# Down products that add to y in PSUM, with y put there by ScalarE or by TensorE, in place of sums on GpSimd

## The chip, the cores and the metric

The kernel runs on one core of one Trainium2 chip. The metric is the device time of one execution in microseconds (us), the median of several runs.

## What is computed

A graph network (two relational convolutions over 625 nodes of 768 features) is followed by a block with 16 experts and one shared network. Only the second part is touched by the change. Cut to what matters:

```python
y = silu(h @ sg_w) * (h @ su_w) @ sd_w            # shared network, 1536 wide
for i in range(16):
    gate_feature = h * pe[i] @ gate_w + gate_b    # 625 x 768
    gate_weight, gate_idx = top_k(gate_feature, 384)
    gate_weight = softmax(gate_weight)
    gathered = take_along_axis(h, gate_idx)
    y = y + (silu((gathered * gate_weight) @ eg_w[i]) * (... @ eu_w[i])) @ ed_w[i]
out = silu(layernorm(y) @ m1_w + m1_b) @ m2_w + m2_b
```

All of it is in float32. The 625 tokens lie as 5 tiles of 125 rows, so y is a tile `y_tok` of 125 x 5 x 768.

## The kernel before

**The sort sets the order.** The top 384 of 768 with what goes with them (the payload: the values of h at those places) come out of a sorting network. The function `experts` runs an OPENING, then 15 REGULAR turns (turn 1 apart, turns 2 to 14 as a hardware loop, turn 15 apart), then a CLOSING. A REGULAR turn has 93 units. In the first 38 or so, units of the new expert's sort of halves alternate with units of the previous expert's merge of the top. In turn 7, the turn that is read most below, unit 0 begins at 3479.6 us. A unit compares two sides of up to 960 columns:

- ScalarE copies the first side into a PSUM bank (`seed`, L1507).
- VectorE takes the larger keys (L1616) and the smaller ones (L1626).
- TensorE subtracts the larger keys from that bank (L1218), so the bank becomes a mask.
- VectorE moves the first payload under the mask (L1649) and the second (L1666). The second one is shared. VectorE moves its part from a saved copy (`pay_side`, made by ScalarE at L1520). For the other part GpSimd adds both sides beforehand (`add_pays`, L1319) and subtracts the new first side afterwards (`take_pays`, L1327).

**How much GpSimd takes** is the function `shares`: half of the payload in a woven unit, 6 of 8 parts where the unit is in `REGULAR.free`, and 3 of 8 in the last units. `REGULAR.free` holds the units beside which GpSimd has nothing else to do, by the list `asked_early` and `asked_late`. The cut goes along the first dimension longer than 1, so where that dimension is 2 the share stays a half whatever is asked.

**Products beside the sort.** While a turn sorts, TensorE also makes 125 x 384 or 128 x 313 products in two PSUM slots (`slots`), spread over the units by their column counts: after the mask of a unit it makes the product parts placed there. The work on a product's result follows one unit later on ScalarE and two later on GpSimd. Engines take their instructions in order, so a long product part delays the next unit's mask. In a loop turn the first half of the units has the 10 down products of the expert before last (`expert_out`: 6 matmuls each, in two parts) and gate products, and the second half the hidden products of the last expert. The shared network is cut in 4 pieces (`piece`): piece 0 in the OPENING, 1 in turn 1, 2 in turn 15, and 3 in the CLOSING and after it. A piece's down products have 3 matmuls each. Turn 15 also holds the down products of experts 13 and 14; those of expert 15 come at the very end.

**y before.** A down product starts at zero. ScalarE copies it out to `y_part`, which lies in `u_feat` (`summed`, L1446), and GpSimd adds that to `y_tok` (`add_to_y`, L1287). There are 10 per expert and 10 per piece, 200 in all. `y_tok` starts from a memset.

Of the kernel before, what the change touches and what calls it, by code (L numbers as in the profile page):

```python
# [819 lines left out]
def experts(nc, ffn, chunks, ident, neg_ident, ones, pe_t, h_tok, h_feat, y_tok, gate_w, gate_b, gate_loaded,  # L820
            m1_loaded):
    with ExitStack() as ctx:
# [3 lines left out]
        def sem(name):  # L826
            return ctx.enter_context(nc.semaphore(name))
# [33 lines left out]

        def is_set(e, t):

            return t < AHEAD and not (isinstance(e, int) and e == 0)
# [30 lines left out]
        y_part = u_feat[:, :, :].rearrange("p k c -> p (k c)")[0:TP, 0:D].rearrange("p (h x) -> p h x", h=2)  # L895
# [14 lines left out]
        hid_ready, y_added = sem("hid_ready"), sem("y_added")  # L910
# [152 lines left out]
        asked_early = [asked(True, parts) for parts in down_parts(KD)]  # L1063
# [52 lines left out]
        def _(pe):  # L1116
# [41 lines left out]
            def down(n, bank, t, half, nf, down_w, loads, hids, part):  # L1158
                if part == 0:
                    if hids is not None:  # L1160
                        pe.wait_ge(hid_ready, hids + 1)
                        pe.wait_ge(down_loaded, loads * 16)
                    room(n)
                for f in range(part * KK, part * KK + KK):
                    last = pe.matmul(slots[bank][0:TP, 0:HALF], hid[:, f, t * TP:(t + 1) * TP],  # L1165
                                     down_w[:, f, half * HALF:(half + 1) * HALF], start=(f == 0), stop=(f == nf - 1))
                if part == nf // KK - 1:
                    last.then_inc(filled, 1)
# [11 lines left out]
            def downs(base, nf, down_w, loads, hids):  # L1180
                return [(down, (base + n, n % 2, t, half, nf, down_w, loads, hids if n == 0 else None), parts)
                        for n, (t, half, parts) in enumerate(halves_of(down_parts(nf)))]
# [8 lines left out]
            def expert_out(e, base):  # L1191
                return downs(base, KD, w_exp, before(e, 1, 1) + 1, before(e, NGU, SGU) + NGU)
# [6 lines left out]
            def piece_out(q, base):  # L1199
                return downs(base + 2 * SGU, KK, w_piece_down, before_piece(q, 1, 1) + 1,  # L1200
                             before_piece(q, NGU, SGU) + SGU)
# [63 lines left out]
        def _(pool):  # L1265
# [32 lines left out]
            def downs(base, nf):  # L1298
                return [(add_to_y, (base + n, t, half), parts) for n, (t, half, parts) in enumerate(halves_of(down_parts(nf)))]
# [4 lines left out]
            def expert_out(base):  # L1304
                return downs(base, KD)

            def piece(base):
                return hiddens(base, KD, KK) + [PAUSE] + downs(base + 2 * SGU, KK)
# [54 lines left out]
            pool.memset(y_tok[:, :, :], 0.0).then_inc(y_added, 1)  # L1363
            pool.wait_ge(y_added, 1)
# [10 lines left out]
            with pool.Fori(2, NEXP - 1) as i:  # L1375
                base = LOOP_BASE + (i - 2) * PER_TURN
                begin_gate(i + 1)
                sort(REGULAR, i, beside_all(
                    REGULAR, expert_out(base) + gate_products(i + 1, range(AHEAD)),
                    expert_in(base + (NHALF + NEARLY)) + gate_products(i + 1, range(AHEAD, NT)), 2))  # L1380
            sort(REGULAR, NEXP - 1, beside_all(REGULAR, expert_out(LAST_BASE) + piece(LAST_BASE + NHALF),
                                               expert_in(LAST_IN) + [PAUSE] + expert_out(LAST_IN + NIN), 2))
# [4 lines left out]
            now(downs(CLOSE_BASE + 2 * SGU, KK))  # L1387
            now(expert_in(END_BASE))
            now(expert_out(END_BASE + NIN))

        @block.scalar
        def _(act):
            def turned(n, bank, ys, t, first, last):
                if t == 0:
                    act.wait_ge(y_added, ys + 1)
# [17 lines left out]
            def with_biases(products):  # L1413


                if products[0][0] is take_feat:
                    for n, bank, _, _, half in [args for _, args, _ in products[0:2]]:
                        set_bias(n, bank, half)
                todo = []
                for n, (work, args, parts) in enumerate(products):  # L1420
                    later = products[n + 2] if n + 2 < len(products) else None
                    if later is not None and later[0] is take_feat and is_set(*later[1][2:4]):
                        todo.append((both, ((work, args), (set_bias, (later[1][0], later[1][1], later[1][4]))), parts))
                    else:
                        todo.append((work, args, parts))
                return todo
# [30 lines left out]
            def downs(base, nf, ys):  # L1457
                return [(summed, (base + n, n % 2, ys, t, half), parts)
                        for n, (t, half, parts) in enumerate(halves_of(down_parts(nf)))]

            def expert_in(e, base):
                turns = [(turned, (base + n, n % 2, before(e, NHALF, NHALF), *place), parts)
# [3 lines left out]
            def expert_out(e, base):  # L1466
                return downs(base, KD, before(e, NHALF, NHALF))
# [4 lines left out]
            def piece_out(q, base):  # L1472
                return downs(base + 2 * SGU, KK, before_piece(q, NHALF, NHALF))
# [101 lines left out]
            for work, args, _ in gate_products(0, NHALF):  # L1575
# [3 lines left out]
            sort(OPENING, 0, beside(OPENING, with_biases(gate_products(1, PIECES) + piece(0, OPEN_BASE)), 1, 1,  # L1579
                                    OPENING.n - 6), REGULAR)  # L1580
            sort(REGULAR, 1, beside_all(
                REGULAR, with_biases(gate_products(2, SECOND_BASE, range(AHEAD)) + piece(1, SECOND_BASE + NEARLY)),
                with_biases(expert_in(0, SECOND_IN) + gate_products(2, SECOND_IN + NIN, range(AHEAD, NT))), 1), REGULAR)
            with act.Fori(2, NEXP - 1) as i:
                base = LOOP_BASE + (i - 2) * PER_TURN
                sort(REGULAR, i, beside_all(
                    REGULAR, with_biases(expert_out(i - 2, base) + gate_products(i + 1, base + NHALF, range(AHEAD))),
                    with_biases(expert_in(i - 1, base + (NHALF + NEARLY))
                                + gate_products(i + 1, base + (NHALF + NEARLY + NIN), range(AHEAD, NT))), 1), REGULAR)
            sort(REGULAR, NEXP - 1, beside_all(  # L1590
                REGULAR, expert_out(NEXP - 3, LAST_BASE) + piece(2, LAST_BASE + NHALF),
# [239 lines left out]
```

## Time and profile before

| what | value |
| --- | --- |
| median of 3 runs | 6728.27 us (6721.94 to 6728.85) |
| span of the profiled execution | 6726.6 us |
| TensorE busy | 5752.0 us, 86% |
| VectorE busy | 5167.5 us, 77% |
| GpSimd busy | 4158.4 us, 62% |
| ScalarE busy | 2659.1 us, 40% |
| first REGULAR turn begins | 1552.4 us |
| last REGULAR turn ends | 6396.5 us |

The profiled execution has no time of its own beside its span, which lies 1.7 us under the median. TensorE's float32 matmuls appear as two records each, so a product of 6 matmuls reads as x12. Matmul ends are modelled, and busy time over the whole span mixes stages with different limits.

### The profile page before, as it was taken

The page shows a single profiled execution, that of the slowest core. Times are in us where ns is not written, and L with a number is a line of the kernel's source. Part 1 is how long each engine was busy: PE and PEld are TensorE (multiplying, and loading weights), DVE is VectorE, ACT ScalarE, POOL GpSimd, SP SyncE. Part 2 cuts the span into 40 slices and gives each one's busy share as a digit, 9 for nine tenths or more (in the row PEclk, how much of TensorE's full clock was granted, in tenths as well). Part 3 has the DMA queues.
Part 4 walks back from the last instruction along what each step waited for, and adds up shares of the span by engine and source line. Part 5 has one row for each costly group of instructions (what it writes and reads, how often), then busy time and mean ns, then how long its engine had stood idle before and what let it go on. Part 6 is the DMA issues. An engine that isn't in the chain of part 4 may idle for free. (4 is left out here: it accounts for less than half of the span.)

```text
span 6726.6 us, 73995 instructions
## 1 busy us (share of the span) xinstructions
PE 5752.0 (86%) x16753; PEld 3063.2 (46%) x16753; DVE 5167.5 (77%) x6633; ACT 2659.1 (40%) x4419; POOL 4158.4 (62%) x3692
## 2 busy tenths in 40 slices
PE   7979989788888888888888888888888888889988
PEld 5545545344444444444444444444444444445554
DVE  3012002399999999999999999999999999998840
ACT  0000000244545554454545454545454545554431
POOL 2325005266877777676777777777777777777740
PEclk9989999899999999999999999999999999999989
DMA  3357238100000000000000000000000000001001
GB/s 90 107 132 188 101 99 196 56 15 8 20 23 15 15 15 15 15 15 15 15 15 14 15 14 15 15 19 10 29 0 29 14 15 15 15 29 36 18 32 51
DMA packets 118084, 261.01 MB, mean 39 GB/s; under 512 B 39164, under 2 KB 49922, under 8 KB 117682
## 3 DMA queue, kind: packets, MB, share of 16 engines
q1 hardware_dynamic: 70322, 180.18, 7.6%
q0 software_dynamic: 47360, 77.17, 5.2%
q14 instruction: 357, 2.92, 0.1%
q8 instruction: 45, 0.74, 0.0%
HBM read 222.43 MB, written 34.58 MB: 38 GB/s over the span
## 5 line engine op out<-in xcount | busy, mean ns | idle before, releaser
L1218 PE MATMUL mask_ps<-key,neg_ident 125*125 125x480 f32 (+7 forms) x4128 | 1886.1, 575 | 567.4 <-DVE key L1626 561.2
L1327 POOL TENSOR_TENSOR pay<-pay_side,pay 125x480 int32<-125x480 int32 (+9 forms) x1120 | 1306.1, 1166 | 648.1 <-DVE pay L1649 641.0
L1507 ACT COPY mask_ps<-key 125x960 f32<-125x960 f32 (+7 forms) x1152 | 954.7, 829 | 1698.7 <-DVE pay L1666 1029.3
L1319 POOL TENSOR_TENSOR pay_side<-pay 125x480 int32<-125x480 int32 (+9 forms) x1120 | 1301.1, 1162 | 340.6 <-DVE pay L1666 160.9
L1218 PEld LDWEIGHTS mask_ps<-key,neg_ident 125*125 125x125 f32 x4128 | 732.8, 192 | 1459.8 <-DVE key L1626 994.5
L1649 DVE COPY_PREDICATED pay<-mask_ps,pay 125x960 f32<-125x960 int32 (+6 forms) x1120 | 1240.7, 1108 | 69.0 <-PE mask_ps L1218 35.5
L1616 DVE TENSOR_TENSOR key<-mask_ps,key 125x960 f32<-125x960 f32 (+6 forms) x1120 | 1092.4, 975 | 57.5 <-PE mask_ps L1218 36.2
L1626 DVE TENSOR_TENSOR key<-mask_ps,key 125x960 f32<-125x960 f32 (+6 forms) x1120 | 1092.8, 976 | 0.0
L1218 PE MATMUL mask_ps<-key_top,neg_ident 125*125 125x480 f32 (+3 forms) x1472 | 604.1, 539 | 178.2 <-DVE key_top L1626 168.0
L1165 PE MATMUL slot_ps<-w_exp,hid 128*125 128x384 f32 x1920 | 680.4, 493 | 8.7 <-issue 8.7
L1153 PE MATMUL slot_ps<-gate_w,xs 128*125 128x384 f32 x1920 | 678.8, 490 | 0.0
L1137 PE MATMUL slot_ps<-u_feat,w_exp 128*128 128x312 f32 (+1 forms) x2304 | 668.2, 427 | 0.4 <-ACT u_feat L1397 0.4
L758 POOL DMA_INDIRECT rows_a<-messages_dram,idx_now_a x200 | 242.3, 1212 | 660.6 <-DVE idx_now_a L795 612.7
L657 PE MATMUL ps_msg<-w_rel,h_feat 128*125 128x384 f32 x1920 | 619.7, 486 | 2.4 <-ACT h_feat L589 2.4
L1666 DVE COPY_PREDICATED pay<-mask_ps,pay_side 125x480 f32<-125x480 int32 (+8 forms) x1120 | 592.1, 529 | 4.8 <-DVE pay L1649 2.9
L1520 ACT COPY pay_side<-pay 125x480 f32<-125x480 f32 (+8 forms) x1120 | 508.6, 454 | 147.0 <-POOL pay L1327 97.6
L1137 PEld LDWEIGHTS slot_ps<-u_feat,w_exp 128*128 128x128 f32 x2304 | 439.7, 191 | 245.0 <-issue 119.0
L668 DVE COPY y_out<-ps_msg 125x768 f32<-125x768 f32 x40 | 38.3, 958 | 612.2 <-PE ps_msg L657 612.2
L1165 PEld LDWEIGHTS slot_ps<-w_exp,hid 128*125 128x125 f32 x1920 | 366.4, 191 | 306.9 <-issue 114.7
L1327 POOL TENSOR_TENSOR pay_top<-pay_side,pay_top 125x480 int32<-125x480 int32 (+3 forms) x272 | 327.5, 1204 | 281.1 <-DVE pay_top L1649 276.8
L1153 PEld LDWEIGHTS slot_ps<-gate_w,xs 128*125 128x125 f32 x1920 | 359.1, 189 | 306.1 <-issue 120.8
L1218 PEld LDWEIGHTS mask_ps<-key_top,neg_ident 125*125 125x125 f32 x1472 | 270.8, 199 | 489.1 <-DVE key_top L1626 289.7
(190 smaller groups left out, 5876.3 us busy)
## 6 DMA issues: line engine op xcount, KB each, us to landing
w_rel<-L_gnn_W SPq DMA_DIRECT2D x16, 2304.0 KB, 23.2
w_exp<-L_ffn_ed_w SPq DMA_DIRECT2D x16, 2304.0 KB, 8.4
messages_dram<-y_out SPq DMA_DIRECT2D x16, 1875.0 KB
w_exp<-L_ffn_eg_w SPq DMA_DIRECT2D x16, 1152.0 KB, 5.4
w_exp<-L_ffn_eu_w SPq DMA_DIRECT2D x16, 1152.0 KB, 7.8
root_w<-L_gnn_root SPq DMA_DIRECT2D x2, 2304.0 KB
w_exp<-L_ffn_sg_w SPq DMA_DIRECT2D x4, 1152.0 KB, 6.0
w_exp<-L_ffn_su_w SPq DMA_DIRECT2D x4, 1152.0 KB, 8.8
```

The source lines that it names most:

```text
L657: last = pe.matmul(slots[n % 2][0:TP, half, 0:HALF], h_feat[:, k, t * TP:(t + 1) * TP], w_rel[j][:, k, cols], start=(k == 0), stop=(k == K ...
L1137: last = pe.matmul(slots[bank][:, 0:count], weight(bank, k), ins[:, k, first:first + count], start=(k == 0), stop=(k == nk - 1))
L1153: last = pe.matmul(slot, xs[:, t % 2, k, :], gate_w[:, k, cols], start=False, stop=(k == KD - 1), skip_group_check=is_set(e, t))
L1165: last = pe.matmul(slots[bank][0:TP, 0:HALF], hid[:, f, t * TP:(t + 1) * TP], down_w[:, f, half * HALF:(half + 1) * HALF], start=(f == 0), ...
L1218: last = pe.matmul(mask, neg_ident[0:TP, 0:TP], operand, start=False, stop=True, skip_group_check=True)
L1319: pool.tensor_tensor(shares(pay_was(turn, u), turn, u)[1].bitcast(I32), first, second, ALU.add).then_inc(pays_added, 1)
L1327: pool.tensor_tensor(second, shares(pay_was(turn, u), turn, u)[1].bitcast(I32), first, ALU.subtract).then_inc(pays_taken, 1)
L1507: act.copy(seed_of(turn, u), compared(turn, u)[0]).then_inc(seeded, 1)
L1616: dve.tensor_tensor(results(turn, u)[0], seed_of(turn, u), compared(turn, u)[1], ALU.max).then_inc(maxed, 1)
L1626: dve.tensor_tensor(smaller, seed, second, ALU.min).then_inc(minned, 1)
L1649: dve.copy_predicated(larger, mask_of(turn, u), second).then_inc(moved, 1)
L1666: dve.copy_predicated(smaller, mask, was).then_inc(pays_done, 1)
```

## The change

A down product now adds onto y in its PSUM slot and ScalarE copies the sum back to `y_tok` (`summed`). How y gets into the slot depends on the product:

- For experts 0 to 13 (`y_is_set`), ScalarE copies y into the slot (`set_y`, L1418 of the changed kernel) right after it has emptied the slot two products earlier. The first two copies of a turn stand ahead of the turn's first unit.
- For pieces 1 to 3 and experts 14 and 15 (`ADDED`), TensorE puts it there by one more matmul at the head of each product: an identity times `y_tok` (L1172).
- Piece 0 (`FIRST`) starts y, so the memset goes.

GpSimd's `add_to_y` is removed, and its entries in `asked_early` no longer keep a unit out of `REGULAR.free`.

```diff
-        y_part = u_feat[:, :, :].rearrange("p k c -> p (k c)")[0:TP, 0:D].rearrange("p (h x) -> p h x", h=2)
...
-        asked_early = [asked(True, parts) for parts in down_parts(KD)]
+        asked_early = [asked(False, parts) for parts in down_parts(KD)]
...
+        def y_is_set(e):
+            return not (isinstance(e, int) and e >= NEXP - 2)
...
                     room(n)
+                    if y is ADDED:
+                        pe.matmul(slot, ident[0:TP, 0:TP], y_tok[:, t, cols], start=True, stop=False)
+                    elif y is not FIRST:
+                        pe.wait_ge(y_set, y + (2 * t + half + 1))
                 for f in range(part * KK, part * KK + KK):
...
+                                     start=(f == 0 and y is FIRST), stop=(f == nf - 1),
...
-            def add_to_y(n, t, half):
-                cols = slice(half * HALF, (half + 1) * HALF)
-                pool.wait_ge(emptied, n + 1)
-                pool.tensor_tensor(y_tok[:, t, cols], y_tok[:, t, cols], y_part[:, half, :], ALU.add).then_inc(y_added, 1)
...
-            pool.memset(y_tok[:, :, :], 0.0).then_inc(y_added, 1)
...
+            def set_y(n, bank, t, half):
+                act.wait_ge(emptied, n - 1)
+                act.copy(slots[bank][0:TP, 0:HALF], y_tok[:, t, half * HALF:(half + 1) * HALF]).then_inc(y_set, 1)
...
-            def summed(n, bank, ys, t, half):
+            def summed(n, bank, t, half, is_y_set):
                 act.wait_ge(filled, n + 1)
-                act.wait_ge(y_added, ys + max(2 * t + half, 1))
-                act.copy(y_part[:, half, :], slots[bank][0:TP, 0:HALF]).then_inc(emptied, 1)
+                act.copy(y_tok[:, t, half * HALF:(half + 1) * HALF], slots[bank][0:TP, 0:HALF]).then_inc(emptied, 1)
```

Ten units of a REGULAR turn enter `REGULAR.free`: 5, 7, 10, 12, 15, 17, 21, 24, 26 and 28. Four of them keep their shapes (5, 7 and 15 are cut along a dimension of 2, and 17 has no second payload). The other six change. VectorE's queue in the loop, at the second payloads of units 24 and 26, stands so before:

```order
L1616 TENSOR_TENSOR key_top<-mask_ps,key_top 125x6x160 [waits mask_made,seeded]
L1666 COPY_PREDICATED pay_top<-mask_ps,pay_side 125x320 [waits moved]
L1626 TENSOR_TENSOR key_top<-mask_ps,key_top 125x6x160 [waits maxed]
L1645 REGISTER_ALU [waits mask_made]
L1647 REGISTER_ALU [waits pay_copied]
L1649 COPY_PREDICATED pay<-mask_ps,pay 125x8x120 [waits pays_added]
L1608 REGISTER_ALU
L1616 TENSOR_TENSOR key<-mask_ps,key 125x8x60 [waits mask_made,seeded]
L1666 COPY_PREDICATED pay<-mask_ps,pay_side 125x4x120 [waits moved]
```

The same piece of VectorE's queue in the changed kernel:

```order
L1626 TENSOR_TENSOR key_top<-mask_ps,key_top 125x6x160 [waits mask_made,seeded]
L1676 COPY_PREDICATED pay_top<-mask_ps,pay_side 125x320 [waits moved]
L1636 TENSOR_TENSOR key_top<-mask_ps,key_top 125x6x160 [waits maxed]
L1655 REGISTER_ALU [waits mask_made]
L1657 REGISTER_ALU [waits pay_copied]
L1659 COPY_PREDICATED pay<-mask_ps,pay 125x8x120 [waits pays_added]
L1618 REGISTER_ALU
L1626 TENSOR_TENSOR key<-mask_ps,key 125x8x60 [waits mask_made,seeded]
L1676 COPY_PREDICATED pay<-mask_ps,pay_side 125x2x120 [waits moved]
```

Nothing has moved. VectorE's second copy of unit 26 goes from 480 to 240 columns, and nothing else in its queue changes but that kind of copy: unit 10 and unit 28 from 240 to 120, units 12, 24 and 26 from 480 to 240, and unit 21 from 320 to 160.

TensorE's queue in turn 15, at down products of expert 14 (`slot_ps<-w_exp,hid`) between masks, before:

```order
L1165 MATMUL slot_ps<-w_exp,hid 125x384 [waits emptied]
L1165 MATMUL slot_ps<-w_exp,hid 125x384 x5
L1218 MATMUL mask_ps<-key,neg_ident 125x4x120 [waits minned]
L1218 MATMUL mask_ps<-key,neg_ident 125x3x120
L1165 MATMUL slot_ps<-w_exp,hid 125x384 [waits emptied]
L1165 MATMUL slot_ps<-w_exp,hid 125x384 x2
```

The same place in the changed kernel:

```order
L1172 MATMUL slot_ps<-y_tok,ident 125x384 [waits emptied]
L1176 MATMUL slot_ps<-w_exp,hid 125x384 x6
L1231 MATMUL mask_ps<-key,neg_ident 125x4x120 [waits minned]
L1231 MATMUL mask_ps<-key,neg_ident 125x3x120
L1172 MATMUL slot_ps<-y_tok,ident 125x384 [waits emptied]
L1176 MATMUL slot_ps<-w_exp,hid 125x384 x3
```

Each product has become one matmul longer, and the mask behind it stands behind that matmul too.

ScalarE's queue at the start of a loop turn, before:

```order
L1507 COPY mask_ps<-key_top 125x640 [waits pays_done]
L1544 REGISTER_ALU
L1496 COPY pay<-h_tok 125x256x5 [waits kept]
L1496 COPY pay<-h_tok 125x128x10 [waits pays_done]
L1496 COPY pay<-h_tok 125x128x10
```

The same place in the changed kernel:

```order
L1418 COPY slot_ps<-y_tok 125x384 [waits emptied]
L1417 REGISTER_ALU
L1418 COPY slot_ps<-y_tok 125x384 [waits emptied]
L1513 ISA
L1514 ISA [waits maxed]
L1516 REGISTER_ALU [waits minned]
L1517 COPY mask_ps<-key_top 125x640 [waits pays_done]
L1554 REGISTER_ALU
L1506 COPY pay<-h_tok 125x256x5 [waits kept]
L1506 COPY pay<-h_tok 125x128x10 [waits pays_done]
L1506 COPY pay<-h_tok 125x128x10
```

Two copies of y now stand ahead of the seed of unit 1 and the three copies that lay out the new payload.

## Rows read from the trace of the kernel before

**Rows 1.** The page, busy tenths of each engine in 40 equal slices.

```profile
DVE  3012002399999999999999999999999999998840
```

**Rows 2.** Turns 2, 7, 15, rest: length, PE PEld DVE ACT POOL busy, clock, DMA.

```profile
1877.80:2195.70 317.90, 268.21 (x753) 136.60 (x753) 307.24 (x372) 159.15 (x267) 235.53 (x207) 0.97 0.04 16
3479.60:3799.50 319.90, 268.45 (x753) 136.55 (x753) 307.15 (x371) 159.02 (x267) 236.53 (x208) 0.96 0.04 15
6045.70:6396.50 350.80, 318.41 (x953) 179.10 (x953) 308.91 (x372) 162.64 (x281) 252.82 (x227) 0.96 0.09 33
6396.50:6726.60 330.10, 275.62 (x881) 168.73 (x881) 91.55 (x110) 76.14 (x136) 75.77 (x77) 0.90 0.10 35
```

**Rows 3.** Waits of VectorE in turn 7, the longest in total: us, times, longest.

```profile
DVE key_top L1616 <- PE mask_ps L1218: 3.6, 2, 2.7
```

**Rows 4.** VectorE's second payload copies in turn 7, by shape.

```profile
L1666 DVE COPY_PREDICATED pay<-mask_ps,pay_side 125x480 f32<-125x480 int32 x17 | 12.0, 704 | 0.0
...
L1666 DVE COPY_PREDICATED pay<-mask_ps,pay_side 125x240 f32<-125x240 int32 x26 | 11.5, 441 | 0.3 <-DVE pay L1649 0.2
...
L1666 DVE COPY_PREDICATED pay<-mask_ps,pay_side 125x120 f32<-125x120 int32 x7 | 2.1, 295 | 0.0
...
L1666 DVE COPY_PREDICATED pay_top<-mask_ps,pay_side 125x320 f32<-125x320 int32 x3 | 1.6, 521 | 0.0
...
L1666 DVE COPY_PREDICATED pay_top<-mask_ps,pay_side 125x160 f32<-125x160 int32 x2 | 0.7, 334 | 0.0
```

**Rows 5.** Timeline of turn 7: TensorE, then VectorE, near units 27 to 29.

```profile
3574.43 1.77 PE L1218 MATMUL mask_ps<-key_top,neg_ident 125*125 125x480 f32 x4
...
3577.05 1.07 PE L1218 MATMUL mask_ps<-key,neg_ident 125*125 125x480 f32 x2 [0.85 <-DVE key L1626]
...
3576.90 1.26 DVE L1649 COPY_PREDICATED pay_top<-mask_ps,pay_top 125x960 f32<-125x960 int32 x1
...
3583.10 1.24 DVE L1649 COPY_PREDICATED pay_top<-mask_ps,pay_top 125x960 f32<-125x960 int32 x1 [0.24 <-issue]
```

**Rows 6.** GpSimd in turn 7, by shape.

```profile
L1327 POOL TENSOR_TENSOR pay<-pay_side,pay 125x480 int32<-125x480 int32 x15 | 18.1, 1204 | 9.1 <-DVE pay L1649 9.1
...
L1327 POOL TENSOR_TENSOR pay<-pay_side,pay 125x720 int32<-125x720 int32 x7 | 11.5, 1649 | 1.5 <-DVE pay L1649 1.5
...
L1287 POOL TENSOR_TENSOR y_tok<-y_tok,u_feat 125x384 f32<-125x384 f32 x10 | 10.0, 1002 | 0.0
```

**Rows 7.** ScalarE's copies out of and into a product slot, turn 7.

```profile
L1446 ACT COPY u_feat<-slot_ps 125x384 f32<-125x384 f32 x10 | 4.8, 478 | 3.7 <-PE slot_ps L1165 3.7
...
L1411 ACT COPY slot_ps<-bias_rows 125x384 f32<-125x384 f32 x8 | 3.9, 483 | 0.7
```

**Rows 8.** Busy time in stretches with down products, columns as in group 2.

```profile
1703.40:1737.90 34.50, 33.71 (x100) 18.50 (x98) 32.74 (x42) 20.11 (x40) 33.07 (x33) 0.98 0.00 1
...
6208.10:6244.30 36.20, 36.13 (x102) 19.93 (x102) 32.52 (x43) 20.93 (x39) 34.30 (x35) 0.92 0.00 1
...
6319.70:6357.60 37.90, 34.17 (x95) 17.02 (x94) 31.09 (x39) 14.12 (x25) 25.08 (x24) 1.00 0.00 1
...
6357.60:6388.10 30.50, 30.50 (x89) 16.27 (x87) 25.11 (x29) 12.22 (x21) 26.20 (x20) 1.00 0.01 2
```

**Rows 9.** Timeline after the last sort: TensorE, then the last two products.

```profile
6494.08 17.25 PE L1165 MATMUL slot_ps<-w_piece_down,hid 128*125 128x384 f32 x48 [6.58 <-ACT u_feat L1446]
...
6604.33 0.48 ACT L1446 COPY u_feat<-slot_ps 125x384 f32<-125x384 f32 x1 [3.39 <-PE slot_ps L1165]
...
6608.20 0.48 ACT L1446 COPY u_feat<-slot_ps 125x384 f32<-125x384 f32 x1 [3.39 <-PE slot_ps L1165]
...
6608.76 0.99 POOL L1287 TENSOR_TENSOR y_tok<-y_tok,u_feat 125x384 f32<-125x384 f32 x1 [2.88 <-ACT u_feat L1446]
```

**Rows 10.** Clock where turns 2 and 7 begin, columns as in group 2.

```profile
1872.00:1892.50 20.50, 12.82 (x20) 5.35 (x19) 17.04 (x21) 12.90 (x16) 8.33 (x7) 0.59 0.00 0
...
3476.30:3496.80 20.50, 12.76 (x18) 5.49 (x19) 15.19 (x17) 12.75 (x16) 6.99 (x6) 0.50 0.01 2
```

More of the change, by code:

```diff
@@ L860, in experts @@
         BEGIN = SCALE + NT
+        FIRST, ADDED = "first", "added"
+        def y_is_set(e):
+            return not (isinstance(e, int) and e >= NEXP - 2)
         def is_set(e, t):
@@ L1156, in gate, with down @@
                     last.then_inc(filled, 1)
-            def down(n, bank, t, half, nf, down_w, loads, hids, part):
+            def down(n, bank, t, half, nf, down_w, loads, hids, y, part):
+                cols = slice(half * HALF, (half + 1) * HALF)
+                slot = slots[bank][0:TP, 0:HALF]
                 if part == 0:
@@ L1163, in down @@
                     room(n)
+                    if y is ADDED:
+                        pe.matmul(slot, ident[0:TP, 0:TP], y_tok[:, t, cols], start=True, stop=False)
+                    elif y is not FIRST:
+                        pe.wait_ge(y_set, y + (2 * t + half + 1))
                 for f in range(part * KK, part * KK + KK):
-                    last = pe.matmul(slots[bank][0:TP, 0:HALF], hid[:, f, t * TP:(t + 1) * TP],
-                                     down_w[:, f, half * HALF:(half + 1) * HALF], start=(f == 0), stop=(f == nf - 1))
+                    last = pe.matmul(slot, hid[:, f, t * TP:(t + 1) * TP], down_w[:, f, cols],
+                                     start=(f == 0 and y is FIRST), stop=(f == nf - 1),
+                                     skip_group_check=y is not ADDED and y is not FIRST)
                 if part == nf // KK - 1:
@@ L1386, in _, with turned @@
                 weigh(NEXP - 1, t)
-            now(downs(CLOSE_BASE + 2 * SGU, KK))
             now(expert_in(END_BASE))
-            now(expert_out(END_BASE + NIN))
         @block.scalar
         def _(act):
-            def turned(n, bank, ys, t, first, last):
-                if t == 0:
-                    act.wait_ge(y_added, ys + 1)
+            def turned(n, bank, t, first, last):
                 act.wait_ge(filled, n + 1)
@@ L1411, in set_bias, with setting, with_settings @@
                 act.copy(slots[bank][0:TP, 0:HALF], bias_rows[:, half * HALF:(half + 1) * HALF]).then_inc(bias_set, 1)
[L1413 to L1418, printed above, removed]
+            def set_y(n, bank, t, half):
+                act.wait_ge(emptied, n - 1)
+                act.copy(slots[bank][0:TP, 0:HALF], y_tok[:, t, half * HALF:(half + 1) * HALF]).then_inc(y_set, 1)
+            def setting(work, args):
+                if work is take_feat and is_set(*args[2:4]):
+                    return [(set_bias, (args[0], args[1], args[4]))]
+                if work is summed and args[4]:
+                    return [(set_y, args[0:4])]
+                return []
+            def with_settings(products):
+                for work, args, _ in products[0:2]:
+                    do(setting(work, args))
                 todo = []
                 for n, (work, args, parts) in enumerate(products):
[L1421 to L1425, printed above, removed]
+                    sets = setting(*products[n + 2][0:2]) if n + 2 < len(products) else []
+                    todo.append((both, ((work, args), *sets), parts) if sets else (work, args, parts))
                 return todo
@@ L1455, in hiddens, with downs @@
                         for n, (place, parts) in enumerate(zip(places, mixed_parts(nk, nf)))]
-            def downs(base, nf, ys):
-                return [(summed, (base + n, n % 2, ys, t, half), parts)
+            def downs(base, nf, is_y_set):
+                return [(summed, (base + n, n % 2, t, half, is_y_set), parts)
                         for n, (t, half, parts) in enumerate(halves_of(down_parts(nf)))]
             def expert_in(e, base):
-                turns = [(turned, (base + n, n % 2, before(e, NHALF, NHALF), *place), parts)
+                turns = [(turned, (base + n, n % 2, *place), parts)
                          for n, (place, parts) in enumerate(zip(TURNS, turn_parts))]
```

44 lines of the change are left out of this document (22 added, 22 removed).

## The prediction, made before the changed kernel ran

> **What bounds the kernel now.** I read the page first. VectorE is busy nine tenths or more in nearly every slice from about 1500 us on [rows 1], and those slices are the 15 REGULAR turns. So I asked for busy time by turn. Turn 7 lasts 319.90 us, of which VectorE is busy 307.15 and TensorE 268.45; turn 15 lasts 350.80 with nearly the same VectorE time, 308.91, but TensorE 318.41; and in the 330.10 us after the last turn VectorE has only 91.55, TensorE 275.62 [rows 2]. The reader should see three regimes. A loop turn goes by VectorE. Turn 15 goes in part by TensorE, and so does the tail. In a loop turn the rest of VectorE's time, 12.75 us, is spent in a few waits; the largest is 3.6 us for masks at two places [rows 3], none of them on GpSimd's sums into y.
>
> **What the change saves on VectorE.** Six second payload copies per turn get shorter. By shape, 480 columns take 704 ns, 240 take 441, 120 take 295, and for the top 320 take 521 and 160 take 334 [rows 4]. Three units save 0.263 us each, two 0.146, one 0.187: 1.27 us per turn. Is all of it gained? Not quite, since TensorE is close behind. In turn 7 it works without a pause from unit 22 until the mask of unit 27, which ends at 3576.20 (3574.43 + 1.77); VectorE uses that mask at 3576.90, 0.70 us later [rows 5]. The savings of units 21, 24 and 26 lie ahead of that instruction and sum to 0.71. I take about 0.2 us as lost there, because a mask's end and its use never lie closer than some 0.2 us in the stretches where VectorE waits. The mask of unit 28 begins 0.85 us after TensorE fell idle, so the pause can take the shift [rows 5]. Unit 28's own 0.146 lies just ahead of an instruction that already waits 0.24 us, at 3583.10 [rows 5], and is lost. That leaves 0.92 us per turn, bounds 0.4 (nothing from units 21 to 28) and 1.27. Thirteen loop turns give 12.0 us, turns 1 and 15, where TensorE paces units 20 to 30, half of that each: **12.9 us gained**, bounds 5.2 and 19.
>
> **What it costs GpSimd and ScalarE.** A GpSimd sum goes from 1204 ns at 480 columns to 1649 at 720 [rows 6], twice per unit. I scale this by columns: the three large units cost 0.9 each, the others about 0.6 each, near 4.5 us per turn. Against that go ten sums into y of 1002 ns, 10.0 us [rows 6]. GpSimd ends 5 us lighter in a turn where it has 83 us of pause [rows 2], so I take nothing. What it costs if the cover fails is a rival below. ScalarE gets ten copies of y into a slot. The nearest row is the bias copied into the same slots, 483 ns; the copy out of it costs 478 and stays [rows 7]. That is 4.8 us per turn on an engine that is busy half of it. A copy of y stands right behind a copy out and ahead of the next seed, which itself waits for VectorE. At a turn's start two copies, 0.97 us, stand ahead of the seed of unit 1 and the three payload copies. VectorE waits there for masks anyway [rows 3]. I take nothing; the lower bound is also nothing, the upper bound 1 us per turn.
>
> **What it costs TensorE.** A down product of expert 15 is paced by TensorE: 6604.33 to 6608.20, 3.87 us for 6 matmuls of 384 columns, 0.645 us each [rows 9]. The added identity matmul has 384 columns too, so 0.645 us. There are 50, in five places:
>
> - Turn 1, piece 1, ten products: TensorE is busy 33.71 of 34.50 us [rows 8]. Ten cost 6.45. The pause of 0.8 and about 1.3 just behind it take some: **4.3** (2.5 to 6.45).
> - Turn 15, piece 2, ten products: 36.13 busy of 36.20 [rows 8], and then hidden products that also fill TensorE. **5.5** (4 to 6.45).
> - Turn 15, expert 14. Its first five products lie in 37.90 us with 34.17 busy, so 3.2 us find 3.73 of pause: nothing. The last five lie in 30.50 us with 30.50 busy [rows 8]: **3.2** (3.2 to 6.45).
> - Piece 3, after the sort: TensorE stands 6.58 us before 6494.08 until ScalarE takes the first results [rows 9]. The first two products are done before that wait, so eight count: **5.2**.
> - Expert 15: ten, behind the load of their weights and ahead of the layer norm, nothing beside them: **6.45**.
>
> The last sum into y disappears: from the end of ScalarE's copy (6608.20 + 0.48) to the end of GpSimd's (6608.76 + 0.99) are **1.1 us gained** [rows 9]. The memset lies where GpSimd waits for TensorE's first transposes: nothing.
>
> **Sum.** 4.3 + 5.5 + 3.2 + 5.2 + 6.45 - 1.1 = 23.5 us of cost, 12.9 of gain, net 10.7 slower. Against the profiled span of 6726.6 that is 6737.3; the median lies 1.7 higher: 6739 us.
>
> **The clock.** Where turn 7 begins, 20.50 us go by at a granted clock of 0.50, the lower level of 1.2 GHz; TensorE is busy only 12.76 of them. Where turn 2 begins it is 0.59 over as long a stretch [rows 10], and turn 2 is 317.90 us long, 2.0 shorter than turn 7, with the same VectorE time [rows 2]. So the phase at which the clock falls and returns is worth about 2 us per turn, and any shift of work may change it. The Trainium skill ("TensorE: Matmul & The Clock Gate", HAM oscillation) says that waits between bursts of matmuls send each next burst off cold. By that rule the added matmuls that follow a wait, such as the first one of expert 15 behind the weight load, would cost twice 0.645, so about 2 us more over the few such places; I leave that in the range.
>
> **The rivals.**
>
> 1. *TensorE hides more, and the gain is whole.* The woven units lose nothing (19 us), turn 1 and piece 2 cost their lower bounds: cost 2.5 + 4 + 3.2 + 5.2 + 6.45 - 1.1 = 20.3, net about +1: 6730. For it: ends of matmuls are modelled, so the 0.70 us may be more. Against: the stretches without a pause [rows 8]. Chance 0.17.
> 2. *The other side: the clock's phase turns in favour of the loop.* If twelve further loop turns take the form of turn 2, each 2 to 3 us shorter, 24 to 36 come off: about 6709. It decides from 24 us on, that is if all twelve gain 2. For it: turn 2 exists [rows 2]. Against: it is the only such turn of 13. Chance 0.10.
> 3. *GpSimd comes late.* With 6 of 8 parts its two sums take 3.3 us in units 24 and 26, of a unit of about 3.5. If the sum then ends after VectorE asks for it in those units, at 0.4 to 0.5 us each for three units, 15 turns lose 20: 6759. For it: little pause there. Against: the y sums leave the same units, and no wait on GpSimd is among the large ones. Chance 0.10.
> 4. *Every added matmul is on the path.* 50 x 0.645 = 32.3, less 2 products hidden at piece 3 and 1.1 at the end, is 29.9; with the gain at 8: +22, so 6750. Chance 0.13.
>
> **How the numbers follow.** The forecast has 0.50 and a range of its own of 6729 to 6751, from the bounds above. A change of 0.2% is 13.5 us, about what a measurement of this kernel can tell from none, so slower begins at 6741.7 and faster ends at 6714.8. Of the forecast's 0.50 about 0.19 lies above 6741.7 and 0.31 below. Slower: 0.19 + rivals 3 and 4, 0.23, is 0.42. Faster: rival 2 and a little of rival 1, 0.12. The rest, 0.46, is no change. The range of 6718 to 6758 leaves out most of rival 2 and half of rival 3.
>
> **What the changed profile would show.** L1676 rows of 240 and 120 columns in six more units, and loop turns shorter by about 1 us. Waits of VectorE on TensorE's masks near units 27 and 29 grow where the savings are lost. 100 records of `slot_ps<-y_tok,ident` (two each) of about 0.32 us of pitch. Turn 1 longer by 3 to 4 us, turn 15 by about 8. After the last turn 330.1 becomes about 341. ScalarE busy some 60 us more, GpSimd about 130 less. The prediction is wrong if loop turns move by 2 us either way, which would be the clock, or if waits on GpSimd's L1327 appear in units 21 to 29.

## The result, and the profile after

The changed kernel takes 6746.68 us (median of 7, 6745.71 to 6752.58), the kernel before 6728.27 (median of 7). The ratio is 1.0032, with a 95% interval of 1.0022 to 1.0043: slower by 15 to 29 us. The prediction had 6739 in a range of 6718 to 6758, with "no change" and "slower" about equally likely.

The profiled execution has a span of 6750.8 us, 24.2 more than before. It was the slowest of the seven, so some 6 us of the 24 are its own. VectorE is 13 us less busy, GpSimd 121 us less, ScalarE 49 and TensorE 46 us more. The page's line of VectorE in 40 slices differs from [rows 1] in one digit.

Busy time of turn 1, of turns 2, 4 and 7, of turn 15, and of the rest, which answers to [rows 2] (start and end, length, busy time of TensorE, its weight loads, VectorE, ScalarE and GpSimd with their counts, granted clock, share of DMA, GB/s):

```profile
1550.90:1880.00 329.10, 289.74 (x858) 158.24 (x857) 307.13 (x372) 162.61 (x279) 236.42 (x203) 0.97 0.04 15
1880.00:2197.40 317.40, 267.06 (x753) 136.32 (x753) 306.17 (x371) 162.77 (x277) 230.89 (x197) 0.97 0.04 16
2518.00:2840.00 322.00, 272.84 (x753) 138.64 (x753) 306.64 (x372) 162.60 (x277) 231.63 (x198) 0.95 0.04 15
3480.90:3801.40 320.50, 270.12 (x753) 137.81 (x753) 306.35 (x371) 162.68 (x277) 231.99 (x198) 0.96 0.04 15
6048.10:6408.30 360.20, 329.70 (x993) 186.36 (x993) 308.09 (x371) 165.54 (x291) 229.59 (x197) 0.96 0.09 32
6408.30:6750.70 342.40, 290.49 (x921) 177.53 (x921) 91.72 (x110) 76.03 (x136) 55.96 (x57) 0.91 0.10 34
```

The reader should see two things. Turn 15 grew by 9.4 us and the rest by 12.3, as forecast in kind. But turn 7, where VectorE has 0.80 us less work (306.35 for 307.15), is 0.6 us longer than before. I take a turn from the start of VectorE's larger keys of its unit 0 to that of the next turn. The 13 loop turns sum to 4168.2 us after and 4167.9 before, so the forecast gain of 12 us in the loop is absent. The rest of the 24.2 us: turn 1 3.7, turn 15 9.4, after the last turn 12.3, loop 0.3, ahead of turn 1 -1.5.

The second payload copies and ScalarE's copies of y in turn 7, by shape, which answer to [rows 4] and [rows 7]:

```profile
L1676 DVE COPY_PREDICATED pay<-mask_ps,pay_side 125x480 f32<-125x480 int32 x14 | 9.7, 694 | 0.0
...
L1676 DVE COPY_PREDICATED pay<-mask_ps,pay_side 125x240 f32<-125x240 int32 x27 | 11.5, 425 | 0.3 <-DVE pay L1659 0.2
...
L1456 ACT COPY y_tok<-slot_ps 125x384 f32<-125x384 f32 x10 | 4.8, 478 | 5.4 <-PE slot_ps L1176 5.4
L1418 ACT COPY slot_ps<-y_tok 125x384 f32<-125x384 f32 x10 | 4.7, 480 | 0.3
```

**Where the loop's gain was first, and where it went.** Units 12 to 30 of turn 8, changed kernel, in the same columns as the turns above:

```profile
3847.90:3905.70 57.80, 53.93 (x156) 27.83 (x155) 56.92 (x74) 27.79 (x50) 43.26 (x34) 1.00 0.11 41
```

The same units of turn 8 in the kernel before:

```profile
3845.70:3904.40 58.70, 54.12 (x156) 27.73 (x155) 58.20 (x74) 26.24 (x45) 45.42 (x41) 1.00 0.11 41
```

So 0.8 to 0.9 us are gained there, in every loop turn. Later in the turn they are lost again at three places; two of them are stretches of low granted clock. Units 55 to 58 of turn 4 and of turn 2, and units 86 to 88 of turn 4 and of turn 5, changed kernel:

```profile
2703.00:2717.70 14.70, 11.77 (x36) 6.74 (x35) 13.73 (x17) 8.99 (x16) 8.96 (x9) 0.88 0.00 1
2062.60:2076.50 13.90, 10.14 (x36) 5.83 (x35) 13.69 (x17) 9.07 (x16) 8.97 (x9) 1.00 0.01 2
...
2810.60:2822.80 12.20, 11.85 (x29) 5.34 (x28) 10.99 (x13) 4.68 (x7) 8.83 (x7) 0.89 0.30 120
...
3132.50:3143.30 10.80, 10.13 (x28) 4.77 (x27) 10.80 (x13) 4.69 (x7) 8.86 (x7) 1.00 0.33 133
```

The work is the same within each pair. Where the granted clock averages 0.88 in place of 1.00, TensorE is 1.6 to 1.7 us longer busy with it, and the stretch is 0.8 to 1.5 us longer. In the profiled execution before, 7 of the 13 loop turns had such a low stretch near unit 55 and none had one near unit 86; after, 12 have the first and 3 the second. With a little at units 4 to 8, where the low stretch of the turn's start lasts 23.9 us in 12 turns (before in 7, and 20.5 us in 5), the clock takes back about 0.6 us a turn. The third place, 0.3 us at units 41 to 45, shows in GpSimd's queue. Its timeline there, turn 7, changed kernel (start, length, instruction, in brackets its idle time and what ended it):

```profile
3618.69 1.44 POOL L1335 TENSOR_TENSOR pay<-pay_side,pay 125x630 int32<-125x630 int32 x1 [0.86 <-DVE pay L1659]
```

VectorE's first payload copy, on which that difference waits, in the same turn:

```profile
3616.96 1.27 DVE L1659 COPY_PREDICATED pay<-mask_ps,pay 125x840 f32<-125x840 int32 x1
```

The copy ends at 3618.23 (3616.96 + 1.27), the difference begins 0.46 us later. At other units this distance is 0.16 us, as it was here before. GpSimd has little pause from there to unit 46, so the 0.3 us pass on to ScalarE's copy and seed, and VectorE waits for that seed.

### The profile page after: what moved, and what is told of

Same layout as the page of the kernel before. It is cut to its first block and busy times, and to the rows that moved or that the text cites. A ratio compares the mean times of both kernels' runs of the same rounds, so it can differ in the third digit from the quotient of the medians.

```text
span 6750.8 us, 73954 instructions
## 1 busy us (share of the span) xinstructions
PE 5797.6 (86%) x16853; PEld 3093.0 (46%) x16853; DVE 5154.4 (76%) x6633; ACT 2708.0 (40%) x4559; POOL 4037.4 (60%) x3491
## 5 line engine op out<-in xcount | busy, mean ns | idle before, releaser
L1335 POOL TENSOR_TENSOR pay<-pay_side,pay 125x480 int32<-125x480 int32 (+9 forms) x1120 | 1336.6, 1193 | 760.2 <-DVE pay L1659 754.0
L1327 POOL TENSOR_TENSOR pay_side<-pay 125x480 int32<-125x480 int32 (+9 forms) x1120 | 1331.7, 1189 | 334.4 <-DVE pay L1676 152.6
L1676 DVE COPY_PREDICATED pay<-mask_ps,pay_side 125x240 f32<-125x240 int32 (+8 forms) x1120 | 575.8, 514 | 4.8 <-DVE pay L1659 2.9
L1530 ACT COPY pay_side<-pay 125x240 f32<-125x240 f32 (+8 forms) x1120 | 496.4, 443 | 138.9 <-POOL pay L1335 89.7
```

Of the source, the lines that this page charges most:

```text
L1327: pool.tensor_tensor(shares(pay_was(turn, u), turn, u)[1].bitcast(I32), first, second, ALU.add).then_inc(pays_added, 1)
L1335: pool.tensor_tensor(second, shares(pay_was(turn, u), turn, u)[1].bitcast(I32), first, ALU.subtract).then_inc(pays_taken, 1)
L1676: dve.copy_predicated(smaller, mask, was).then_inc(pays_done, 1)
```

## The experiments

Each comes with the median of its runs and the ratio to the kernel before, with its 95% interval. Ratios are against runs of the kernel before on the same chip, whose medians were 6725.9 to 6727.1 us. The profile of each is one of its executions, and the turns are read from that one. The table behind the experiments puts the turns side by side.

**The two halves of the change, apart.** First the y part alone:

```diff
-        asked_early = [asked(False, parts) for parts in down_parts(KD)]
+        asked_early = [asked(True, parts) for parts in down_parts(KD)]
```

> The changed kernel with the free list of the kernel before: y still goes through PSUM, but the six units keep their old shares. Theory A (my reading of the trace after): each loop turn of the changed kernel is 0.81 us shorter in units 12 to 31 by the shares alone, so they become 0.8 us longer, 13 x 0.81 + about 1 for turns 1 and 15 = 11.5 us, 6747 + 11.5 = about 6758 us; the pause of GpSimd of 0.3 us ahead of its difference in unit 40 stays, since it belongs to the number of instructions in GpSimd's queue and not to the shares, so units 41 to 45 stay at 15.6 us. Rival (GpSimd is late by its larger shares, the forecast's third rival in small): units 41 to 45 go back to the 15.34 us of before, and the kernel is only about 7 us slower than the changed one.

Measured: 6750.63 us, ratio 1.0042 (1.0028 to 1.0056). Units 12 to 30 went back to the lengths of before, so the 0.8 us there are the shares' own. Units 41 to 45 stayed at 15.7 us: the pause at unit 40 has nothing to do with the shares. But the loop grew by only 2.3 us in place of 10.5, against both readings: low stretches near unit 55 stand in 3 of the 13 turns now, where the changed kernel has them in 12.

Then the share part alone, the same line of the kernel before changed from True to False:

> The kernel before with GpSimd's share raised in the six units and its ten sums into y kept beside them. Theory A (VectorE gains what its shorter copies save, GpSimd is not late by its sums): units 12 to 31 shorter by 0.81 us per loop turn, units 41 to 45 at 15.34 us as before, 6728 - 11 = about 6717 us. Rival B (GpSimd cannot carry both): in units 24 and 26 its two payload sums take 3.0 to 3.3 us and the sum into y 1.0, more than the unit of 3.1 to 3.8; its difference comes up to 0.7 us late there and VectorE waits for ScalarE's copy behind it: half or more of the gain goes, 6723 to 6735 us.

Measured: 6727.39 us, ratio 1.0002 (0.9993 to 1.0012). Neither was right. GpSimd carries both: units 12 to 30 are 0.8 us shorter in every turn, as in this row of turn 8:

```profile
3845.80:3903.60 57.80, 53.90 (x156) 27.83 (x155) 56.96 (x74) 25.55 (x45) 49.65 (x41) 1.00 0.12 41
```

The gain is whole there and gone at the end of the turn, and units 41 to 45 are at 15.3 us in 8 of 13 turns. What takes it is low stretches near units 40, 55 and 86, which add 0.1, 0.2 and 0.5 us to the mean turn. So the vanished gain is not a cost of the y part.

**GpSimd's pause at unit 40.** Two empty instructions in place of each removed sum:

```diff
+            def filler():
+                for _ in range(2):
+                    pool.engine_nop()
...
-                return [(nothing, (), parts) for parts in down_parts(nf)]
+                return [(filler, (), parts) for parts in down_parts(nf)]
```

> The changed kernel with two empty instructions in GpSimd's queue at each place where a sum into y was, so that its queue has as many instructions per turn (590) as before. Theory A (a pause of 0.3 us stands at fixed counts of GpSimd's queue, at units 17 and 40 now, at 52 and 90 before, and only at 40 is it on the path): it goes back to units 52 and 90, units 41 to 45 take 15.34 us in place of 15.63, 13 x 0.3 = 4 us faster than the changed kernel: about 6743 us. Rival (the 0.3 us at unit 40 come from what GpSimd or ScalarE does before): nothing moves, 6747 us.

Measured: 6749.52 us, ratio 1.0038 (1.0025 to 1.0052). The place in GpSimd's timeline:

```profile
3623.68 1.44 POOL L1339 TENSOR_TENSOR pay<-pay_side,pay 125x630 int32<-125x630 int32 x1 [0.54 <-DVE pay L1663]
```

The idle time is 0.54 us in place of 0.86, and units 41 to 45 take 15.35 us in 9 of the 13 loop turns (15.75 where a low stretch lies on them). The pause left unit 40, but it did not go back to units 52 and 90 as the theory had it: there, too, the difference begins 0.16 us behind the copy. So its place does not go by the number of instructions alone, which is 590 again. And the time did not follow: the loop is 4168.3 us, as before the edit. That is a second 0.3 us per turn that VectorE saved for nothing.

**TensorE's added matmuls.** Two of ten products per piece or expert by the identity, the other eight by ScalarE (the first two follow products of 313 columns in their slots, so I kept a matmul that begins the slot anew there):

```diff
-                    if y is ADDED:
+                    if y is not FIRST and 2 * t + half < y[1]:
                         pe.matmul(slot, ident[0:TP, 0:TP], y_tok[:, t, cols], start=True, stop=False)
...
-                return downs(base + 2 * SGU, KK, False)
+                return downs(base + 2 * SGU, KK, NHALF if q == 0 else 2)
```

> The changed kernel, but in pieces 1 to 3 and experts 14 and 15 only the first two products of ten get y by TensorE's identity matmul, the other eight by ScalarE: 40 of the 50 added matmuls are gone, 40 more copies of 0.48 us on ScalarE. Theory A (the added matmuls are on the path at 0.6 us each wherever TensorE has no pause): turn 1 gets back 3.3 of 4.1 us, turn 15 some 7 of 9.4, piece 3 its 4.9, expert 15 5.2 of 6.45, sum about 20 us: 6727 us. Rival (ScalarE's second copy between two products of a slot delays TensorE, above all at products of three matmuls, 1.94 us): half of it or less, 6737 us or more.

Measured: 6728.57 us, ratio 1.0002 (0.9993 to 1.0011), so 18 us came back. In the profile turn 1 is 325.5 us (329.0), turn 15 352.1 (360.2), and the rest:

```profile
6391.80:6721.90 330.10, 278.63 (x889) 169.61 (x889) 91.67 (x110) 83.93 (x152) 56.03 (x57) 0.91 0.10 35
```

330.1 us is what the kernel before has there [rows 2]. ScalarE's copies cost nothing that shows, not even between products of three matmuls.

**More and less work on VectorE.** Two kernels were to add work to VectorE in the kernel before:

```diff
                 for u in range(max(turn.streams, 1), turn.n):
+                    if turn is REGULAR and u == 50:
+                        for n in range(2):
+                            dve.tensor_copy(spare[:, :], h_mixed[:, n * 384:(n + 1) * 384])
```

> The kernel before with two more copies of 384 columns in VectorE's queue ahead of unit 50 of every REGULAR turn (about 0.4 us each, 0.8 to 0.9 in sum). In the four kernels tried so far and in the two given, turns 3 to 14 of the loop had a mean of 320.7 to 320.9 us, whatever VectorE saved; the turns without a low clock near 189 or 292 us were 319.8 to 320.4. Theory A (the low clock takes up what VectorE saves, and gives back what it adds): the mean of turns 3 to 14 stays at 320.8 to 321.2 us, the kernel within 4 us of before. Rival (VectorE's work adds up as in the sum of the prediction): 15 x 0.85 = 13 us slower, mean turn 321.7.

> The kernel before with six such copies per turn (about 2.5 us). Rival (plain addition): 15 x 2.5 = 38 us slower, mean turn 323.3. Theory A: the low clock can give back at most what it takes beyond the fixed 20.5 us at a turn's start, about 1.0 us of the mean turn, so some 1.5 us per turn come through, 22 us or more slower, unless the turns settle at a next common length.

Measured: 6726.18 us (1.0003) and 6727.0 us (1.0002). These say nothing on either theory. A REGULAR turn never runs that loop, and the traces have no instruction on `spare`: both were the kernel before once more. They show how far the same program varies: a loop of 4167.5 and 4171.0 us beside 4167.9, a mean of turns 3 to 14 of 320.8 and 321.1 us, and 1544 to 1552 us ahead of turn 1.

Less work: five copies cut to a quarter of their columns. This kernel leaves out exchanges, so it computes something else and serves only to measure:

```diff
+                    if turn is REGULAR and u in (33, 35, 37, 49, 60):
+                        smaller, mask, was = [side[:, 0:side.shape[1] // 4] if side.shape[1] > 3 else side[:, :, 0:side.shape[2] // 4]
+                                              for side in (smaller, mask, was)]
                     dve.wait_ge(moved, turn.done("moves", i, u + 1))
```

> The kernel before with VectorE's second payload copies of units 33, 35, 37, 49 and 60 cut to a quarter of their columns (three quarters of these copies are left out, so the payloads of these places are not exchanged). VectorE has about 2.3 us less work per turn. Rival (plain addition): 15 x 2.3 = 35 us faster, mean turn 318.5. Theory A: the low clock takes back about 1 us or more of it per turn; 10 to 20 us faster at most, mean turn 319.5 to 320.8.

Measured: 6682.01 us, ratio 0.9938 (0.9924 to 0.9952). That is 32 to 51 us faster, which excludes the 10 to 20 us of theory A and holds plain addition (35). The turns go further than plain addition, whose mean turn was 318.5 us. Turn 7:

```profile
3458.80:3776.20 317.40, 267.98 (x753) 136.40 (x753) 304.83 (x371) 159.11 (x267) 236.48 (x208) 0.97 0.04 15
```

VectorE is 2.3 us less busy than in [rows 2], turns 3 to 14 lie between 317.4 and 317.7 us, and none of them has a low stretch but the one at its start. The loop fell by 41.4 us, 30 of them VectorE's work and 11 the low stretches that are gone.

Theory A was then put anew: call the length that a loop turn has with no low stretch but that at its start its quiet length. Between a quiet length of about 317.4 and 320.8 us further low stretches come in just so many turns that the mean is 320.8. The real addition to VectorE's work, in the loop that runs:

```diff
                 for u in range(1, turn.streams):
+                    if turn is REGULAR and u == 50:
+                        for n in range(2):
+                            dve.bn_stats(spare[:, 6 * n:6 * n + 6], h_mixed[:, n * HALF:(n + 1) * HALF])
```

> The kernel before with two more instructions in VectorE's queue ahead of unit 50 of every REGULAR turn (statistics of 384 columns each, 0.47 us: 0.94 us a turn, results unused). A turn of before with no low clock but that at its start takes 319.8 us, the mean is 320.8. Theory A (as long as such a turn is between 317.4 and 320.8 us, low stretches come until the mean is 320.8): such a turn now takes 320.7 us, the mean stays at 320.8 to 321.1, the kernel within 5 us of before. Rival (plain addition): 15 x 0.94 = 14 us slower, mean turn 321.8.

Measured: 6727.09 us, ratio 0.9999 (0.9990 to 1.0008). The two instructions are there in all 15 turns:

```profile
L1682 DVE BATCH_NORM_STATS2 spare<-h_tok x30: 516/542/576, 1725.3 to 6239.7; 125x6 f32<-125x384 f32 x30
```

Turn 10 is typical:

```profile
4447.00:4767.80 320.80, 268.88 (x753) 136.87 (x753) 308.09 (x374) 158.98 (x266) 236.84 (x208) 0.96 0.04 15
```

VectorE works 0.9 us more a turn and the kernel is as fast as before, in 11 runs. Plain addition, 14 us, lies outside the interval, and so do the 9 us that the quiet length alone would give, which grew by 0.6 us (VectorE waits 0.3 us less near unit 55). What is given back shows in the clock: no turn has a low stretch near unit 55, where 7 had one before. The profiled execution was the slowest of the 11 (6738.78 us), so its loop of 4174.5 us is probably longer than that of most. And four of them:

> The kernel before with four of the unused statistics of e9_plus_1 per turn (1.88 us). A turn with no low clock but that at its start would take 319.8 + 1.9 = 321.7 us, beyond the length of 320.8 at which the turns of before settle. Theory A (there is a next such length, 3.4 us up, as 320.8 is 3.4 above 317.4): mean turn 324.2 us, 13 x 3.4 + about 4 for turns 1 and 15 = 48 us slower, 6775 us. Rival 1 (the low clock only takes up what is left below 320.8, and above it the work is added plainly): mean turn 321.7 to 322.0, 16 to 20 us slower, 6745 us. Rival 2 (plain addition to the mean of before): 322.7, 28 us slower, 6755 us.

Measured: 6751.38 us, ratio 1.0042 (1.0028 to 1.0055), mean turn 323.3 us. That is 19 to 37 us slower. It excludes the 48 us of theory A and holds rival 2 (28 us), with rival 1 (16 to 20) at its edge. By the turns none of the three is right: the mean lies between plain addition (322.7) and a settled length of 324.2, turns 3 to 14 vary from 321.5 to 325.1, and 6 of the 13 have a low stretch near unit 86, where before none has. Two such instructions cost nothing, four cost 24 to 28 us.

**Filling TensorE's pauses at a turn's start:**

```diff
+            def idle(base, count):
+                room(base)
+                for _ in range(count):
+                    pe.matmul(slots[0][0:TP, 0:HALF], ident[0:TP, 0:TP], h_mixed[:, 0:HALF], start=True, stop=True)
...
+                for spot, count in {90: 2, 91: 2, 92: 4, 0: 3, 1: 3}.items():
```

> The kernel before with matmuls whose results nobody reads (384 columns, 0.645 us each) in TensorE's pauses at the end and the start of a loop turn: 2, 2 and 4 behind the masks of units 90, 91 and 92, 3 and 3 behind those of units 0 and 1. Theory A (the clock falls at a turn's start because TensorE pauses there): the 20.5 us at 0.50 shrink or go, the masks of units 0 and 2 take 1.8 us in place of 3.6, VectorE waits 2 to 3 us less per turn: 13 x 2.5 = about 30 us faster, 6695 us. Rival (the clock falls anyway, or falls a little later): the added matmuls themselves run at the half clock and stand ahead of the masks: same or up to 20 us slower.

Measured: 6723.91 us, ratio 0.9998 (0.9989 to 1.0007). Units 0 to 3 of turn 5:

```profile
2831.80:2848.90 17.10, 13.39 (x35) 6.69 (x34) 14.35 (x16) 9.49 (x12) 4.81 (x4) 0.90 0.00 1
```

The granted clock is 0.90, where units 0 to 3 of turn 5 stand at 0.50 and take 17.9 us in the kernel before (compare [rows 10]), so the low stretch at a turn's start does come from TensorE's pauses. The rule on oscillation that the prediction cites from the Trainium skill ("TensorE: Matmul & The Clock Gate", HAM oscillation) agrees with this. It saves 0.8 us in these units, not 2.5, and nothing at the end: turns now range from 319.0 to 324.4 us, the latter with low stretches at units 75 to 88, and their mean is 320.9.

**Past the edge.** Seven more units at the larger share, once on the kernel before with its sums on GpSimd, once on the changed kernel with the edits of e3 and e4:

```diff
-                        and all(work is nothing for work, _ in asking.get(u, []))}
+                        and all(work is nothing for work, _ in asking.get(u, []))} | {61, 66, 69, 71, 73, 83, 85}
```

> The kernel before (y summed by GpSimd) with GpSimd's share raised in the six units of the change and in seven more (61, 66, 69, 71, 73, 83, 85). VectorE saves 0.81 + 7 x 0.27 = 2.7 us a turn, so a turn with no low clock but that at its start would take 317.1 us. Theory A (the mean turn is either 320.8 or 317.4 us, and drops to the lower once such a turn is below 317.4): mean turn 317.4, 13 x 3.4 = 44 us faster than before, about 6683 us. Rival 1 (plain addition of what VectorE saves): 15 x 2.7 = 40 us, 6687 us with turns of differing length. Rival 2 (GpSimd is late with 13 units at the larger share): little or nothing, 6720 us or more.

> The changed kernel with the same seven units at the larger share, with only two of ten products by the identity matmul as in e4_two_added, and with the empty instructions of e3_filler in GpSimd's queue. Theory A: the mean turn drops to 317.4 us as in e10_more_before, the rest as in e4_two_added: about 6683 to 6686 us. Rival (y by ScalarE costs something that only a loop free of low stretches shows): 10 us or more behind e10_more_before.

Measured: 6684.02 us, ratio 0.9933 (0.9919 to 0.9946), and 6686.42 us, ratio 0.9942 (0.9928 to 0.9955). Both are faster than the kernel before and the changed one. Turn 7 of the first:

```profile
3458.80:3775.60 316.80, 266.26 (x753) 135.74 (x753) 304.24 (x372) 157.77 (x267) 247.48 (x208) 0.97 0.04 16
```

GpSimd carries 11 us more than in [rows 2] and isn't late. The mean turn is 318.0 us, not 317.4, and the loop's 36.3 us less are close to plain addition (35), so by the time alone the two theories can't be told apart here. What can be told is that the first 0.8 us of savings bring nothing (e2) and the next 1.9 us bring 36. The two ways for y give the same time within their spread.

**The turns side by side.** The quiet length is worked out: that of before, 319.8 us, with the differences of the units' lengths that each edit makes. The mean is that of turns 3 to 14 of the profiled execution.

| kernel | quiet length | mean turn | 13 loop turns | ratio |
| --- | --- | --- | --- | --- |
| e10, e11 | 317.1 | 318.0, 318.1 | 4131.6, 4132.6 | 0.9933, 0.9942 |
| e7 | 317.4 | 317.5 | 4126.5 | 0.9938 |
| e2, e8 | 319.0 | 320.9, 320.9 | 4168.6, 4169.0 | 1.0002, 0.9998 |
| e3 | 319.0 | 320.9 | 4168.3 | 1.0038 |
| changed | 319.3 | 320.9 | 4168.2 | 1.0032 |
| e4 | 319.3 | 320.7 | 4167.5 | 1.0002 |
| before | 319.8 | 320.8 | 4167.9 | 1 |
| e1 | 320.1 | 320.7 | 4170.5 | 1.0042 |
| e9 | 320.4 | 321.0 | 4174.5 | 0.9999 |
| e12 | 321.3 | 323.3 | 4199.8 | 1.0042 |

Over 1.4 us of quiet length, 319.0 to 320.4, the mean stays within 0.3 us, which is as much as it varies between executions of the kernel before (320.8, and 320.8 and 321.1 in e5 and e6). The cost of the added matmuls (changed, e1, e3) lies outside the loop and shows in the ratio alone.

## Why the prediction was right, and what it got wrong

- **The gain of 12.9 us** is the step that failed. Its first half held: VectorE's copies got shorter as costed, unit 28 gained nothing, and 0.3 us were lost near unit 27 (0.2 forecast), which leaves 0.8 us a turn (0.92 forecast). The 0.2 rested on the reading that a mask's end and its use never lie closer than that; over the whole trace before, VectorE's 128 waits on masks show 0.10 to 0.70 us, with a median of 0.19. But the sum took a turn to be shorter by what its units save, and in the loop it is not: e2 made the saving alone and the loop kept its length, e9 added 0.9 us and kept it too. The section on the clock saw that its phase is worth 2 us a turn, put it in the range and gave it 0.10 as a piece of luck. It is not luck: in the kernels between 319.0 and 320.4 us of quiet length it worked against the change, whichever sign that had.
- **GpSimd and ScalarE at nothing**: right. In turn 7 GpSimd is 4.5 us lighter (5 forecast) and ScalarE 3.7 us busier (4.8). Not foreseen was a pause of 0.3 us in GpSimd's queue, which stands at unit 40 when the sums have left the queue (changed kernel and e1) and not when empty instructions fill their place (e3).
- **TensorE's cost of 23.5 us**: right in sum, and each term within 1.1 us. Piece 1 4.1 us (units 41 to 54 of turn 1; 4.3 forecast), piece 2 5.1 (5.5), expert 14 4.3 (3.2; its first five products, which were to fit into pauses of 3.73 us, cost 1.1), piece 3 4.9 (5.2), expert 15 with the sum that goes 5.3 (6.45 - 1.1 = 5.35): 23.7. The last product of expert 15 shows how it reads:

```profile
6626.26 0.81 PE L1172 MATMUL slot_ps<-y_tok,ident 125*125 125x384 f32 x2
6626.91 4.04 PE L1176 MATMUL slot_ps<-w_exp,hid 128*125 128x384 f32 x12
```

  6626.91 - 6626.26 is 0.65 us, as priced. e4 took 40 of the 50 away and got 18 us back. Another 2.2 us after the last turn are 3.4 us of low clock at 6694.2 us, in the output stage, that the trace before has not. The section on the clock left about 2 us more for the added matmuls that follow a wait. The first product of expert 15, behind an idle time of 8.67 us:

```profile
6582.67 1.61 PE L1172 MATMUL slot_ps<-y_tok,ident 125*125 125x384 f32 x2 [8.67 <-issue]
6584.07 6.20 PE L1176 MATMUL slot_ps<-w_exp,hid 128*125 128x384 f32 x12
```

  6584.07 - 6582.67 is 1.40 us, so this one did run at the low clock, about twice 0.645. But it adds little: TensorE's start of the ten products and ScalarE's last copy out of them lie 6.4 us further apart than before (6582.67 to 6631.0, against 6566.27 to 6608.2), which is ten times 0.64. The low stretch was there before too, and the added matmul took the place of another in it.
- **The sum.** 23.7 of cost less nothing, beside 18 to 21 us measured over all runs: the number 6739 came out 8 us low because a gain was counted that isn't there. The range held it. (The upper bounds of its terms add up to 6753, not the 6751 stated, which decides nothing.)
- **The rivals.** The first (the gain is whole) was wrong, the second (the clock turns in favour of the loop) had the right place with the wrong sign: the clock does decide the loop's length, but it took the gain instead of adding one; the third (GpSimd late in units 24 and 26) did not occur, even with the sums of y kept beside (e2). The fourth (all matmuls on the path) came nearest in time, for another reason.

What stays open is why the low stretches settle the mean at 320.8 us: the runs show that they come and go with the quiet length, not what sets the places at which the clock falls. e12 shows that there isn't simply a second such length 3.4 us above the first, and e10 and e11 (318.0 and 318.1 us) that the mean isn't simply 317.4 below it. And it wasn't tried whether ScalarE could set y for all ten products.

## What to carry to other kernels

Where a loop's turns differ in length though their work doesn't, look at the granted clock stretch by stretch before you sum small savings: here 0.8 us a turn bought nothing, 0.9 us more cost nothing, and 2.3 and 2.7 us saved brought 41 and 36 us in the loop. A saving that is measured as "no change" may be half of one that pays: try it together with the next. In this kernel a matmul that only brings an operand into PSUM cost its full 0.65 us wherever TensorE had no pause, while ScalarE, half idle, made the same copies, two per product, without a cost that shows.

## What the runs showed of the hardware

- Copies of 384 columns by ScalarE took 480 ns into PSUM (L1418) and 478 out of it (L1456), so here neither way was the cheaper.
- In GpSimd's queue a pause of about 0.3 us stands at certain places of every loop turn: the difference begins 0.45 us behind the copy that it waits for, in place of 0.16, at units 52 and 90 before and at 17 and 40 after. With two empty instructions for each sum that went, no difference shows it, neither at 17 and 40 nor at 52 and 90 (e3). What sets the places was not found.
- Matmuls without use at a turn's start raised the clock there from 0.50 to 0.90 (e8). Low stretches came at other places instead, such as units 75 to 88, and the kernel's time stayed.
